# A fused clustering layer and channel gate on one core: column norms through four column groups, totals on VectorE, GpSimd's chain work at the close of its step

## The reference, cut to what matters

```
x = x + cluster(groupnorm(x))
x = x + gate(groupnorm(x))

cluster(v):                       # per image, 8 heads, 2 x 2 regions of 64 x 64 pixels
  y       = Wp v + bp             # per head 32 point and 32 value channels
  centres = means of y over an 8 x 8 grid of blocks in the region     # 64 centres
  sim     = sigmoid(alpha * cos(point, centre) + beta)                # 4096 pixels x 64 centres
  best, m = argmax, max of sim over the centres
  agg[s]  = (centre value + sum of m * value over pixels with best = s) / (1 + sum of m)
  out     = Wm (m * agg[best]) + bm

gate(v): v * sigmoid(w2 relu(w1 (mean over the DCT terms of v)))      # one factor per channel
```

## Time and profile before

| what | value |
|---|---|
| median of 3 runs | 4753.57 us (4753.42 to 4755.43) |
| profiled execution | 4749.32 us, of which the span of the trace is 4747.4 us |
| TensorE matmul busy | 4436.3 us (93%) |
| TensorE weight loads busy | 4259.2 us (90%) |
| VectorE / ScalarE / GpSimd busy | 3599.6 / 3326.7 / 3219.1 us (76 / 70 / 68%) |
| granted TensorE clock, mean | 0.98 |

### The profile page before, as it was taken

One profiled execution on the slowest core, in us unless ns is written; L12 is line 12 of the kernel. 1 busy time (PEld: TensorE's weight loads), 2 busy tenths in 40 slices (PEclk: granted clock), 3 DMA queues, 4 the chain that ended last, 5 costly groups with the idle time before them and its releaser, 6 DMA issues.

```text
span 4747.4 us, 141619 instructions
## 1 busy us (share of the span) xinstructions
PE 4436.3 (93%) x51792; PEld 4259.2 (90%) x51792; DVE 3599.6 (76%) x7894; ACT 3326.7 (70%) x8843; POOL 3219.1 (68%) x3519
## 2 busy tenths in 40 slices
PE   2888999999999999999999999999999999999992
PEld 2788999999999999999999999999999999999982
DVE  5766778887887878887788878887788777777763
ACT  5766677777777777777777767777777776666652
POOL 2555666676777777777777767777777777777762
PEclk8999999999999999999999999999999999999996
DMA  5544455586877778777777767777678776666668
GB/s 182 126 100 110 113 121 129 136 189 165 186 189 186 181 169 189 184 189 178 174 189 181 190 164 182 190 186 187 162 187 191 186 167 145 155 150 156 155 153 261
DMA packets 1823073, 798.83 MB, mean 168 GB/s; under 512 B 1629216, under 2 KB 1629616, under 8 KB 1822384
## 3 DMA queue, kind: packets, MB, share of 16 engines
q1 hardware_dynamic: 1822384, 789.77, 68.7%
HBM read 395.15 MB, written 260.05 MB: 138 GB/s over the span
## 4 chain that ended last, share of the span: by engine, by line
PE 70%; POOL 13%; issue 6%; POOLq 4%; ACT 3%; DMA 2%; SPq 1%; DVE 1%; ACTq 0%; DVEq 0%
PE bank L1136 48%; PE bank L1302 8%; PE bank L1244 6%; PE bank L1289 4%; POOL xl L722 3%; PE bank L1275 3%; POOL vals L729 2%; POOL dl L736 2%; POOL vpart L676 2%; POOL fin L682 2%; DMA out<-fin 1%; DMA chunk<-x 1%; ACT xh L874 1%; ACT ysq L865 1%; POOLq L579 0%
## 5 line engine op out<-in xcount | busy, mean ns | idle before, releaser
L722 POOL TENSOR_TENSOR xl<-xr,xh 128x512 fp32r<-128x512 f32 x512 | 654.7, 1279 | 584.4 <-ACT xh L874 569.9
L729 POOL TENSOR_TENSOR vals<-vals,vpart 128x528 f32<-128x528 f32 x512 | 614.8, 1201 | 519.2 <-ACT vpart L915 519.1
L1036 DVE TENSOR_TENSOR gath<-bank,mv 128x512 f32<-128x512 f32 x503 | 347.9, 692 | 622.9 <-PE bank L1244 622.0
L1021 DVE TENSOR_REDUCE rank<-bank 128x8 f32<-128x512 f32 x1024 | 694.8, 690 | 94.4 <-PE bank L1136 81.5
L849 ACT ACTIVATE yh<-bank,bpf 128x256 fp32r<-128x256 f32 x1024 | 428.4, 469 | 364.6 <-PE bank L1136 363.7
L1136 PE MATMUL bank<-xh,wph 128*128 128x256 f32 x2048 | 583.8, 285 | 92.7 <-POOL xl L722 58.8
L1046 DVE TENSOR_TENSOR hot<-bank,rank 128x512 bf16<-128x512 f32 x1024 | 655.6, 682 | 0.0
L676 POOL TENSOR_TENSOR vpart<-vals,vpart 128x528 bf16<-128x528 f32 x512 | 611.6, 1194 | 64.6 <-ACT vpart L843 64.5
L736 POOL TENSOR_TENSOR dl<-dsq,dh 128x512 fp32r<-128x512 f32 x503 | 649.6, 1291 | 6.6 <-ACT dsq L917 6.4
L889 ACT ACTIVATE dh<-bank 128x512 fp32r<-128x512 f32 x503 | 299.8, 596 | 481.8 <-PE bank L1275 481.5
L1136 PE MATMUL bank<-ch,yh 128*128 128x256 f32 x2048 | 620.9, 303 | 0.0
(11 more groups left out here) (204 smaller groups left out, 13241.6 us busy)
## 6 DMA issues: line engine op xcount, KB each, us to landing
xr<-x SPq DMA_DIRECT2D x1024, 128.0 KB, 2.5
mixed<-xr SPq DMA_DIRECT2D x480, 256.0 KB, 2.6
chunk<-x SPq DMA_DIRECT2D x448, 256.0 KB, 3.9
fin<-mixed SPq DMA_DIRECT2D x448, 256.0 KB, 3.8
out<-fin SPq DMA_DIRECT2D x896, 128.0 KB, 3.4
xr<-x SPq DMA_DIRECT2D x64, 256.0 KB, 6.6
hot_t<-hot SPq DMA_TRANSPOSE x1024, 2.5
out<-hot_t SPq DMA_DIRECT2D x18, 512.0 KB, 6.0
```

Of the source, the lines that this page charges most:

```text
L722: pool.tensor_tensor(xl[:, G0 % 2], xr[:, G0 % SLOTS], xh[:, G0 % 2].bitcast(F32), ALU.subtract).then_inc(s_xl, 1)
L729: pool.tensor_tensor(vals[:, G2 % 2], vals[:, G2 % 2], vpart[:, 0], ALU.subtract).then_inc(s_r1, 1)
L1021: op = V.tensor_reduce(rank[:, t], sims[t], axis=AX.X, op=ALU.max)
L1036: V.tensor_tensor(g_out.rearrange("p (a c) -> p a c", c=CH) if J1 >= late and J1 % 2 else gath[:, :].rearrange("p (a c) -> p a c", c=CH), ...
```

## The change

It has six parts.

1. Norms (stage 7): weights and moving operand change places. The weights are 32 columns of `hsum` (every fourth of the 128), the 128 columns of `ysq` are moved, and each of the four products is written to its own 32 partitions, so to its own column group. The result lies transposed, heads by pixels, as 128 x 128.
2. VectorE's clamp, Ln and Exp therefore run on 128 columns in place of 16, Exp writes `rnorm` in SBUF, and a new matmul with `rnorm` as weights and 16 columns of `ident` turns the result back, after the products with the centres. ScalarE clears the 16 columns in PSUM beforehand (a Copy of `nothing`), since the matmul adds onto them.
3. The totals of a region are summed on VectorE from PSUM (`totals`); `hold_totals` on ScalarE and the additions on GpSimd go.
4. GpSimd's chain work moves from the middle of its step to the end, behind `dl`.
5. Links of the chain move by a step or more, and TensorE's with them; bands are scaled in the steps 1, 2, 5, 7, 9, 11, 13 and 15 of each 16.
6. SP stores a band before it loads the next.

```diff
@@ -87,19 +87,21 @@
-        return [(n, i - (PER * n - 16)) for n in range(1, N) if 0 <= i - (PER * n - 16) < 16]
+        return [(n, i - (PER * n - 17)) for n in range(1, N) if 0 <= i - (PER * n - 17) < 17]
...
-        return [(n, i - start[n]) for n in range(N) if 0 <= i - start[n] < 7]
-
-    SCALE0 = PER + ADD + 8
+        return [(n, i - start[n]) for n in range(N) if 0 <= i - start[n] < 10]
+
+    SCALE0 = PER + 2 * GROUPS
+    SCALED = (1, 2, 5, 7, 9, 11, 13, 15)
...
-        return [(n, (i - PER * n - SCALE0) // 2) for n in range(N - 1)
-                if 0 <= i - PER * n - SCALE0 < 2 * BANDS and (i - PER * n - SCALE0) % 2 == 0]
+        return [(n, (i - PER * n - SCALE0) // GROUPS * len(SCALED) + SCALED.index((i - PER * n - SCALE0) % GROUPS))
+                for n in range(N - 1) if 0 <= i - PER * n - SCALE0 < 2 * BANDS
+                and (i - PER * n - SCALE0) % GROUPS in SCALED]
...
@@ -124,8 +126,8 @@
-        rnorm = sb("rnorm", [P, TILES * HEADS])
-        lnn = sb("lnn", [P, TILES * HEADS])
+        rnorm = sb("rnorm", [P, P])
+        nothing = sb("nothing", [P, TILES * HEADS])
...
@@ -335,7 +338,7 @@
-        fold_links, gate_links = (2, 6, 7, 8, 9), (2, 4, 5)
+        fold_links, gate_links = (2, 7, 8, 9, 10), (3, 6, 7)
...
@@ -449,8 +452,6 @@
-                for n, b in scale_at(i + 2):
-                    load_band(n * BANDS + b, n, b, n * BANDS + b - 2)
...
@@ -460,6 +461,8 @@
+                for n, b in scale_at(i + 2):
+                    load_band(n * BANDS + b, n, b, n * BANDS + b - 2)
...
@@ -587,14 +586,6 @@
-                pool.wait_ge(s_tread, upto(R))
-                pool.tensor_tensor(total, held[:, :, 0], held[:, :, 1], ALU.add)
-                pool.drain()
-                pool.tensor_tensor(total, total, held[:, :, 2], ALU.add)
-                pool.drain()
-                pool.tensor_scalar(den[:, :, :], total[:, :, CH:CH + 1], 1.0, None, ALU.add).then_inc(s_den, 1)
-                pool.tensor_tensor(aggf[:, :, :], total[:, :, 0:CH], cvd[:, n % 2, r], ALU.add)
-                pool.drain()
...
@@ -682,41 +673,6 @@
-                for n, link in fold_at(i):
-                    if link == 0:
-                        pooled_blocks(n)
...
-                if (i - 19) % GROUPS == 0 and 0 <= R < 4 * N:
-                    table_mean(R)
...
-                if (i - 20) % GROUPS == 0 and 0 <= R < 4 * N:
-                    table_rest(R)
...
@@ -735,6 +691,41 @@
+                for n, link in fold_at(i):
+                    if link == 0:
+                        pooled_blocks(n)
...
+                    if link == 8:
+                        squared_centres(n)
...
+                if (i - 19) % GROUPS == 0 and 0 <= R < 4 * N:
+                    table_mean(R)
...
+                if (i - 20) % GROUPS == 0 and 0 <= R < 4 * N:
+                    table_rest(R)
...
@@ -810,11 +801,6 @@
-
-            def hold_totals(R):
-                act.wait_ge(s_agg, upto(R * GROUPS + GROUPS - 1))
-                nc.scalar.activation(held.rearrange("p k q c -> p (k q c)"),
-                                     a_ps.rearrange("p k c -> p (k c)"), ACT.Copy, scale=keep_s).then_inc(s_tread, 1)
...
@@ -856,9 +842,8 @@
-                R = (i - 19) // GROUPS
-                if (i - 19) % GROUPS == 0 and 0 <= R < 4 * N:
-                    hold_totals(R)
+                    act.wait_ge(s_agg, upto(G2 - 2))
+                    nc.scalar.activation(r_ps[G2 % 2], nothing[:, :], ACT.Copy).then_inc(s_rz, 1)
...
@@ -920,7 +905,7 @@
-                    nc.scalar.activation(lnn[:, :], rnorm[:, :], ACT.Ln, scale=LN_SCALE)
+                    nc.scalar.activation(rnorm[:, :], rnorm[:, :], ACT.Ln, scale=LN_SCALE)
...
@@ -932,10 +917,9 @@
-                    act.wait_ge(s_agg, upto(G1 - 2))
-                    nc.scalar.activation(r_ps[G1 % 2], lnn[:, :], ACT.Exp, scale=-0.5, bias=lnbias).then_inc(s_rn, 1)
+                    nc.scalar.activation(rnorm[:, :], rnorm[:, :], ACT.Exp, scale=-0.5, bias=lnbias).then_inc(s_re, 1)
...
-                    if link == 2:
+                    if link == 3:
...
@@ -964,6 +948,10 @@
+            V.memset(nothing[:, :], 0.0)
+            for b in range(2):
+                V.memset(r_ps[b], 0.0)
+            dve.drain().then_inc(s_r0, 1)
...
@@ -995,6 +983,22 @@
+
+            def totals(R):
+
+                n, r = R // 4, R % 4
+                dve.wait_ge(s_agg, upto(R * GROUPS + GROUPS - 1))
+                dve.wait_ge(s_tab, upto(R - 1))
+                if n and r == 0:
+                    dve.wait_ge(s_cen, upto(n))
+                V.tensor_reduce(total, a_ps.rearrange("p k (q c) -> p k c q", q=PARTS), axis=AX.X, op=ALU.add
+                                ).then_inc(s_tread, 1)
+                dve.wait_ge(s_tread, upto(R))
+                V.tensor_scalar(den[:, :, :], total[:, :, CH:CH + 1], keep_s, 1.0, ALU.mult, ALU.add
+                                ).then_inc(s_den, 1)
+                V.scalar_tensor_tensor(aggf[:, :, :], total[:, :, 0:CH], keep_s, cvd[:, n % 2, r], ALU.mult, ALU.add)
+                dve.wait_ge(s_den, upto(R))
+                V.reciprocal(den[:, :, :], den[:, :, :]).then_inc(s_rec, 1)
...
@@ -1050,23 +1054,23 @@
-                    dve.wait_ge(s_den, upto(R))
-                    V.reciprocal(den[:, :, :], den[:, :, :]).then_inc(s_rec, 1)
+                    dve.wait_ge(s_rz, upto(min(G2, NG - 1)))
+                    totals(R)
...
@@ -1093,7 +1097,8 @@
-                    V.tensor_scalar(rnorm[:, :], n_ps[:, 0:TILES * HEADS], NORM2_MIN, None, ALU.max).then_inc(s_nc, 1)
+                    dve.wait_ge(s_rn, upto(G1 - 1))
+                    V.tensor_scalar(rnorm[:, :], n_ps[:, 0:P], NORM2_MIN, None, ALU.max).then_inc(s_nc, 1)
...
@@ -1129,6 +1134,8 @@
+
+            pe.wait_ge(s_r0, 1)
...
@@ -1218,6 +1225,10 @@
                         op.then_inc(s_sim[t], 1)
+                    pe.wait_ge(s_re, upto(G2))
+                    pe.wait_ge(s_rz, upto(G2 - 2))
+                    mm(r_ps[G2 % 2], rnorm[:, :], ident[:, 0:P:CH // HPM], start=False, stop=True,
+                       skip_group_check=True).then_inc(s_rn, 1)
                 if on(G1):
...
@@ -1276,7 +1287,7 @@
-                    pe.wait_ge(s_z, upto(min(G3 + 1, NG - 1)))
+                    pe.wait_ge(s_rz, upto(min(G3 + 1, NG - 1)))
...
@@ -1298,9 +1309,9 @@
                         for m in range(M):
-                            c = HEADS * t + HPM * m
-                            op = mm(n_ps[:, c:c + HPM], ysq[:, m, t * P:(t + 1) * P], hsum[:, :, 0], start=True,
-                                    stop=True)
+                            rows = CH * (M * t + m)
+                            op = mm(n_ps[rows:rows + CH, 0:P], hsum[:, :, :].rearrange("p a b -> p (a b)")[:, 0:P:HPM], ysq[:, m, t * P:(t + 1) * P],
+                                    start=True, stop=True)
                     op.then_inc(s_n2, 1)
...
```

More of the change, by code:

```diff
@@ L31 @@
 FIRST = 12
-SIGS = 24
+SIGS = 22
 def upto(index, each=1):
@@ L59, in cluster_block @@
     BLOCKS = H // CS
-    STEPS = NG + ADD + 9
+    STEPS = NG + ADD + 12
     xf = x.rearrange("n (k p) h w -> n p k h w", p=P)
@@ L230, in cluster_block @@
         s_nc = sem("norms_guarded")
-        s_rn = sem("norms_inverted")
+        s_re = sem("norms_inverted")
+        s_rn = sem("norms_transposed")
+        s_rz = sem("norms_cleared")
+        s_r0 = sem("norms_cleared_at_first")
         s_z = sem("argument")
@@ L684, in _ @@
                     op.then_inc(s_scaled, 1)
-                for n, link in fold_at(i):
-                    if link == 0:
-                        pooled_blocks(n)
-                    if link == 2:
[L689 to L706, removed]
-                    if link == 3:
-                        gate_input(n)
-                    if link == 6:
-                        gate_scale(n)
-                R = (i - 19) // GROUPS
-                if (i - 19) % GROUPS == 0 and 0 <= R < 4 * N:
-                    table_mean(R)
-                R = (i - 20) // GROUPS
-                if (i - 20) % GROUPS == 0 and 0 <= R < 4 * N:
-                    table_rest(R)
-                R = (i - 1 + CENTRE_LEAD) // GROUPS
-                if (i - 1 + CENTRE_LEAD) % GROUPS == 0 and R < 4 * N and R % 4:
-                    centres_low(R)
                 if on(G0):
@@ L737, in _ @@
                                        ALU.subtract).then_inc(s_dl, 1)
+                for n, link in fold_at(i):
+                    if link == 0:
+                        pooled_blocks(n)
+                    if link == 2:
+                        read("fold", n, 0)
+                        variance(gst1, var1, tm1, s_var)
+                    if link == 4:
+                        group_rstd(n)
+                    if link == 7:
+                        kept_bias(n)
+                    if link == 8:
+                        squared_centres(n)
+                    if link in (12, 13, 14):
+                        normalised(n, link - 12)
```

(25 more changed lines are left out.)

26 lines of the change are left out of this document (10 added, 16 removed).

## The result

| | median us | runs | ratio to before, 95% interval |
|---|---|---|---|
| before | 4753.49 (4751.91 to 4755.43) | 4 | 1 |
| after | 5222.76 (5217.04 to 5226.73) | 4 | 1.0986 (1.0967 to 1.1005) |
| predicted | 5052 (4965 to 5150) | | 1.063 |

A forecast was written before the change was run, and what follows sets the result against it. TensorE bounds the kernel before; the new wait closes a ScalarE-TensorE loop. Its 489 steps total 4585 us, 279 more; with 10 for the first steps and 10 for the clock, 4749.3 + 279 + 20 = 5048, as median 5052 (4965 to 5150).

The forecast's parts named there:

- the loop that was listed: dh, vpart, dsq, chunk, Ln, Exp, turn back, y, gather, values, mixing, transposes, dh: 9.12 us with a chunk, 8.50 without.
- The norms: TensorE's norms in the new form: 0.48 us a step taken, from 0.25 to 1.05, against 0.98 removed.
- the 0.6 with a further drain: TensorE's norms nearer to 0.6 us if changing the tiling mode buys a further drain per step.
- the upper case (no overlap, 1.05): Rival on TensorE's norms: column groups run one after the other, 1.05 us; 4850 us, or 5065 in the loop; 3%.
- Wider Ln and Exp: ScalarE's Ln and Exp on 128 columns: 0.09 and 0.12 us more, together 0.22 (0.1 to 0.3).
- Turning back: TensorE from Exp's end to y's start, the product with rnorm included: 0.36 us (0.25 to 0.55).
- TensorE alone at 8.10: TensorE's step without the wait for Exp: 8.36 - 0.5 + 0.24 = 8.10 us.
- The first rival: TensorE stays the bound: -0.26 us a step, -133 us, plus gains from GpSimd's order; 4520 to 4570 us; 6%.
- The table: The gather waits for the table's second part, now behind dl on GpSimd: 1.4 us, 31 times, 43 us.
- TensorE from y's start until dh can start: Last part of the loop, on TensorE, read from the kernel before: 5.62 us.
- the 15 that I had added here: TensorE's next-image products under the same wait: 1.0 us too much, about two an image, seven images, 15 us.
- The faster rival's second half: Moving GpSimd's chain behind xl gives back 50 to 100 us of irregular steps; in the rival given 6%.

The follow-up runs named there:

- e1: Kernel after, with the product that turns the norms back moved behind y's matmuls: 4760.31 us, ratio 0.9997.
- e2: Kernel before, with only a wait for ScalarE's Exp added ahead of y: 4931.40 us, ratio 1.0356.
- e3: Kernel after, with ScalarE's square of the chunk moved from ahead of Ln to behind Exp: 5001.99 us, ratio 1.0512.
- e10: Kernel after, product behind y as in e1, table_rest at the front of GpSimd's step, 64 unused bytes a partition behind zero: 4649.02 us, ratio 0.9774.
- e6: Kernel after, with an unused buffer of 64 bytes a partition behind zero, no instruction changed: 5184.09 us, ratio 1.0893.
- e9: Kernel after, with norms, Ln and Exp as in the kernel before, and 64 unused bytes a partition behind zero: 4801.82 us, ratio 1.0096.
- e7: Kernel before, with an unused buffer of 64 bytes a partition behind zero, no instruction changed: 4829.53 us, ratio 1.0152.
- e8: Kernel before, with an unused buffer of 128 bytes a partition behind zero: 4761.53 us, ratio 1.0011.
- e12: Kernel before, with 64 unused bytes a partition behind wpl and 64 behind wml: 4757.90 us, ratio 1.0004.

## Why the prediction was right and where it failed

Right, with the runs that show it:
- *The mechanism.* The wait ahead of y closes the loop that was listed. e1 takes the wait off y and 447 of the loop's 462 us are back; e2 puts it alone into the old kernel and pays 175; e3 takes the chunk out of the loop and gains 0.61 in a usual step.
- *The norms*: 0.39 us, taken as 0.48; the 0.6 with a further drain is too much as well, and the upper case (no overlap, 1.05) is excluded. They are off the chain.
- *Wider Ln and Exp*: 0.30 and 0.40 us, as worked out. *Turning back*: 0.30 from Exp's end to y's start, taken as 0.36.
- *TensorE alone at 8.10*: 8.16 in e1, 8.06 in e10. The first rival's step comes out where y isn't held; its time, 4520 to 4570, no run reaches.
- *The table*: 1.65 us a time by the waits (51.3 / 31), taken as 1.4.

The loop's miss is 183 us (462 against 279). It can be split by the parts of the loop, summed over the 489 steps of the trace:

| part of the loop | my sum, us | measured, us |
|---|---|---|
| dh's start to Exp's end | 1603 | 1636 |
| Exp's end to y's start | 176 | 165 |
| y's start to the next dh | 2806 | 2967 |

**The step that failed is the last: "TensorE from y's start until dh can start: 2412.30 - 2406.68 = 5.62".** It was carried over from the kernel before as if TensorE's blocks had a fixed length, and as if every step were the usual one. Measured, it is 5.82 in the usual step, and the whole part is 161 us over my sum. What the runs show in its place:
- *A slower pace of the float32r matmuls*, from buffer addresses that the change moves: 46 us of this part come back in e6 (2967 to 2921), 39 us of the whole. The new size of rnorm did this, 448 bytes more a partition, which is 64 over a multiple of 128; I priced it at nothing.
- *y starts cold.* In the kernel before y usually follows the products with the centres at their pace. Here it stands behind a wait and the f32 product, and its second start comes at 2406.81 - 2406.61 = 0.20. With the addresses put back (e6) the usual step still has 5.70 us here against 5.61 before: 0.09 x 489 = 44 us. e2 shows that a wait alone does it: its second start comes at 0.22, and this part grows by 35 us over the kernel before. I had put 0.07 a step for this into the 0.36 that came out at 0.30.
- *The totals and the table.* VectorE's totals hold vals, which ScalarE has ahead of dh: the step is 0.83 us longer here, 25 us in 31 steps. I had 18 for them in the first part. The table's steps cost 59 us, where I had 43.
- *The clock.* By the trace's clock records the loop has 133 us at the lower of the two levels, before had 61. If TensorE worked all through the further 72, they cost half of it, 36 us; I had 10, outside this term. No run separates it from the rest.

These come to 46 + 44 + 25 + 16 + 36 = 167 us, and the 15 that I had added here for TensorE's products for the next image go off, since those stand ahead of y: 152 of the 161. The items overlap where a long step is also one at the lower clock, so this is an estimate, and only the first two rest on a run of their own.

In the first part, dh to Exp, the sum was 33 us short, and the reason stands in the kernel before. There the same part takes 1530 us, where my rows, without what the change adds, come to 1477: my list of ScalarE's work between dh and Exp was incomplete. The change itself added 106 us to it, where I had 126.

The range failed because it allowed an error of 0.15 us a step, and the miss was 0.37. Nothing in it was set aside for TensorE's own length, which was taken as known.

The faster rival's second half, gains from GpSimd's new order, no run shows. Where y isn't held and the norms are the old ones (e9) the new order and the totals cost 46 us, and the waits show the table. With the table early and the norms new (e10) the usual step is 0.30 us shorter than before, which over 489 steps would be 147 us; 107 are gained.

## What to carry to other kernels

A product that waits for another engine belongs behind the largest block that doesn't need it: the same two instructions cost 462 us more ahead of y than behind it. Before an engine's block is carried into a new sum as a constant, ask what started it at pace and which addresses its operands have; a changed buffer size is an edit of every buffer behind it, and is tested with an unused one. When an experiment that leaves an engine's instructions alone changes their duration, look at where the data lies.

## What the runs showed of the hardware

- 64 bytes of unused buffer slow a TensorE-bound kernel by 1.5% (e7), 128 by 0.1% (e8): with the 64, y's matmuls of 128 x 256 float32r start every 0.120 us instead of every 0.113.
- The half of 128 bytes is not all: a third pace of 0.118 appeared in blocks whose own operands hadn't moved (e12), and more often after a wait alone (e2).
- The second float32r matmul of y starts 0.20 to 0.22 us after the first behind a wait (after, e2), and 0.12 behind it where y follows the products with the centres without one.
- Eight f32 matmuls of 128 columns in four column groups keep the next block back by 0.39 us.
- After the same stop of 1.8 us TensorE went on at the lower clock in e6 (0.86 granted for the step) and at full clock in the kernel after (1.00), image after image; in other steps it is the kernel after that falls to 0.86. What decides it is open.
